# The sparse front of a graph and expert kernel: one-hots, keys, shifts and layer norm rewritten

## The reference

```python
edge_index = stack([src, dst])              # 41250 edges, sorted by dst; 1250 nodes
x = x + gnn(layernorm(x), edge_index, ...)  # x: 1250 x 512
x = x + moe(layernorm(x), ...)              # 512 tokens, 8 experts, 2 of them each

def gcn_conv(x, W, b, src, dst, n):
    h = x @ W.T
    s, d = concat(src, arange(n)), concat(dst, arange(n))   # own loop added
    deg = zeros(n).at[d].add(1.0); dinv = deg ** -0.5
    out = segment_sum(h[s] * (dinv[s] * dinv[d])[:, None], d, n)
    return out + b
# gnn: gcn_conv(512->128), relu, gcn_conv(128->64), then a decoder 64->128->256->512
# layernorm: (x - mean) / sqrt(var + 1e-5), no scale and no shift
```

## Time and profile before

| | us |
|---|---|
| median of 3 runs | 245.8 (245.12 to 248.06) |
| profiled execution | 245.55 |
| its span, first to last instruction | 243.8 |

### The profile page before, as it was taken

The page is one execution under the profiler, slowest core; times in us unless marked ns, Lnnn a source line. Parts: engine busy times, 40 slices in busy tenths (PEclk is TensorE's granted clock), DMA queues, the critical chain, the costliest instruction groups (busy, mean ns, idle before and its releaser), DMA issues.

```text
span 243.8 us, 3869 instructions
## 1 busy us (share of the span) xinstructions
PE 193.7 (79%) x1297; PEld 146.8 (60%) x1303; DVE 146.5 (60%) x292; ACT 105.0 (43%) x224; POOL 39.3 (16%) x50
## 2 busy tenths in 40 slices
PE   2371579999998888799999999978999999993000
PEld 2371369999997777765575544435977777771000
DVE  2919995766769881596560226865398667541224
ACT  3823974766743342630150342702587666440000
POOL 8600000000000000000010060057334400000750
PEclk9999999999999998589999999997799999999555
DMA  5999995000000000000000000424223921113573
GB/s 140 360 285 372 368 365 178 3 0 3 0 3 0 0 0 4 4 3 0 3 0 3 0 3 0 153 80 126 82 56 118 307 93 56 56 63 104 157 219 143
DMA packets 16011, 23.82 MB, mean 98 GB/s; under 512 B 3086, under 2 KB 7952, under 8 KB 15988
## 3 DMA queue, kind: packets, MB, share of 16 engines
q1 hardware_dynamic: 14354, 18.64, 22.9%
q0 software_dynamic: 1536, 4.72, 7.0%
q10 hardware_dynamic: 98, 0.17, 0.2%
HBM read 17.29 MB, written 6.23 MB: 96 GB/s over the span
## 4 chain that ended last, share of the span: by engine, by line
PE 71%; DVE 11%; DMA 7%; issue 5%; POOL 3%; ACT 1%; POOLq 1%; ACTq 0%; DVEq 0%
PE bank L1196 14%; PE bank L1266 11%; PE bank L1405 10%; PE bank L1432 5%; PE bank L1178 4%; PE bank L1191 4%; PE bank L1416 3%; PE bank L1435 3%; PE bank L1376 3%; PE bank L1417 2%; POOL at L526 2%; PE bank L1167 2%; DVE at L553 2%; DMA at<-y_rows,slot_i 2%; DVE ring L597 2%
## 5 line engine op out<-in xcount | busy, mean ns | idle before, releaser
L1196 PE MATMUL bank<-ring 128*128 128x120 bf16 x324 | 42.8, 290 | 0.0
L1196 PEld LDWEIGHTS bank<-ring 128*128 128x128 bf16 x324 | 35.2, 118 | 3.2 <-issue 0.6
L597 DVE TENSOR_TENSOR ring<-iota_quad,src_lo 128x1024 bf16<-128x1024 f16 x41 | 28.3, 690 | 13.9 <-PE bank L1202 13.3
L958 ACT CAST at<-bank 128x440 f32 (+1 forms) x41 | 21.9, 534 | 25.0 <-PE bank L1202 23.9
L1266 PE MATMUL bank<-at,ring 128*128 128x512 bf16 (+1 forms) x145 | 29.4, 345 | 0.5 <-issue 0.4
L597 DVE TENSOR_TENSOR ring<-iota_quad,key 128x960 bf16<-128x960 f16 x41 | 26.7, 651 | 0.0
L1191 PE MATMUL bank<-zeros_bf,ident_bf 128*128 128x440 bf16 (+1 forms) x41 | 15.3, 372 | 13.0 <-DVE ring L597 11.7
L1405 PE MATMUL bank<-at_r 128*128 128x512 f32 (+1 forms) x64 | 21.8, 404 | 0.0
L805 DVE TENSOR_TENSOR ew_r<-ew,at_r 128x1024 fp32r<-128x1024 f32 x16 | 19.3, 1216 | 0.0
L498 POOL MEMSET ring<- 128x640 bf16 x1 | 0.6, 632 | 114.3 <-PE bank L1272 114.3
L1266 PEld LDWEIGHTS bank<-at,ring 128*128 128x128 bf16 x150 | 13.6, 100 | 9.1 <-issue 1.1
(11 more groups left out here) (174 smaller groups left out, 346.3 us busy)
## 6 DMA issues: line engine op xcount, KB each, us to landing
ew<-in_w SPq DMA_DIRECT2D x16, 512.0 KB, 9.8
x_sb<-in_x SPq DMA_DIRECT2D x9, 256.0 KB, 4.9
out<-x_sb SPq DMA_DIRECT2D x9, 256.0 KB, 2.9
y_rows<-at SPq DMA_DIRECT2D x8, 256.0 KB, 2.1
wd3t_sb<-in_Wd3T SPq DMA_DIRECT2D x1, 512.0 KB, 5.3
x_rows<-xn SPq DMA_DIRECT2D x1, 512.0 KB, 2.8
x_rows<-at SPq DMA_DIRECT2D x1, 512.0 KB, 3.5
y_rows<-at SPq DMA_DIRECT2D x8, 64.0 KB, 2.3
```

Of the source, the lines that this page charges most:

```text
L597: last = v.tensor_tensor(hot[:, slot], lanes_quad[:, a:a + n].unsqueeze(1).to_broadcast([P, QUADS, n, QUAD]), of.rearrange("p (q t) -> p q ...
L958: nc.scalar.copy(at[:, :, bass.ds(column, wide)], bank[j][:, 0:CH * wide].rearrange("p (c n) -> p c n", c=CH)).then_inc(s_placed, 1)
L1196: last = mm(acc[:, :, bass.ds(shifts[g], WINDOW)], hot_src[:, j, t // QUAD, :, t % QUAD], hot_dst[:, j, t // QUAD, :, t % QUAD], start=Fal ...
```

## The change

It rewrites the work from the edges to `dinv`.

- One-hots are dense: one row of 128 or 80 elements per tile. Keys are held twice in a row (`lo2`, `key2`), so that comparisons read pairs.
- `WINDOW` is 8, each tile has its own shift, `WIDE` is 40, the last batch's 48. The first tile product starts the bank (`start=True`), without a product of zeros, except in the last batch. `at` is no longer cleared.
- Keys are made in rows by DVE as bf16 (`lo_row`, `key_row`, `carry_row`) and transposed by bf16 products; ACT and DVE spread them from PSUM. The first destinations of tiles are loaded by two DMAs of 4-byte pieces (`next_first`, `first_i`), which give shifts and columns.
- The checks for the general path are spread over POOL, DVE, ACT and PE.
- Layer norm is folded: the raw x is transposed and projected with weights whose column means are taken off (`w1c`, with a column of ones that gives the sum of x); ACT takes one sum of squares in place of two passes and a normalisation; the root of the variance is joined to that of the degree, and `h` is scaled with both (`norm_col`).
- 32 batches are unrolled, with a feature chunk for every three of them.
- `spread_dinv` runs inside the first aggregation, behind its first part. PE warms up with 16 products in place of 40.

```diff
-    WINDOW = 12
+    WINDOW = 8
-    WIDE = 44
-    WIDE_LAST = 2 * WINDOW
+    WIDE = 40
+    WIDE_LAST = 48
-    HEAD = 24
+    HEAD = 32
+    TRANSPOSED = [1 + 3 * c for c in range(CH)]
+    PROJECTED = [3 + 3 * c for c in range(CH)]
+    CENTRED = 2
...
 @block.sync
+            sp.dma_start(next_first[0:ROWS - 1, :],
+                         dst[rowlen:(ROWS - 1) * rowlen + 1:rowlen].rearrange("(r a) -> r a", a=1),
+                         allow_slow_non_contiguous=True).then_inc(s_next, 16)
...
 @block.gpsimd
-            nc.gpsimd.memset(at_flat, 0.0).then_inc(s_at_zero, 1)
...
 @block.vector
+            i_src, i_dst = edges[:, 0, :], edges[:, 1, :]
+            dve.wait_ge(s_src, 32)
+            link(v.tensor_scalar(hi_row, i_src, 0x1F80, 4, ALU.bitwise_and, ALU.logical_shift_right))
+            v.scalar_tensor_tensor(lo_row, hi_row, -16.0, i_src, ALU.mult, ALU.add).then_inc(s_lo_row, 1)
+            dve.wait_ge(s_dst, 32)
+            dve.wait_ge(s_next, 16)
+            v.tensor_copy(first_f[:, 0:ROWT], i_dst[:, 0:rowlen:P]).then_inc(s_first_f, 1)
...
+            for t in range(ROWT):
+                v.scalar_tensor_tensor(key_row[:, t * P:(t + 1) * P], i_dst[:, t * P:(t + 1) * P], first_f[:, t:t + 1],
+                                       hi_row[:, t * P:(t + 1) * P], ALU.subtract, ALU.add).then_inc(s_key_row, 1)
...
+                for hot, of, n, a in ((hot_src, lo, P, 0), (hot_dst, key, COLS, first)):
+                    last = v.tensor_tensor(hot[:, slot].rearrange("p t (n a) -> p t n a", a=2),
+                                           iota_slots[:, a:a + n].rearrange("p (n a) -> p n a", a=2).unsqueeze(1)
+                                           .to_broadcast([P, BATCH, n // 2, 2]),
+                                           of.unsqueeze(2).to_broadcast([P, BATCH, n // 2, 2]),
                                            ALU.is_equal)
...
+                    link(keep_keys(SOON, ROWS))
+                    dve.wait_ge(s_carryT, 1)
...
+                if b == 1:
+
+                    v.tensor_tensor(falls[:, 0:rowlen - 1], i_dst[:, 1:rowlen], i_dst[:, 0:rowlen - 1],
+                                    ALU.is_lt).then_inc(s_falls, 1)
...
+                if b == CENTRED:
+                    dve.wait_ge(s_colsum, 1)
+                    v.scalar_tensor_tensor(w1c[:, :, 0:HID], bank[7][:, 0:HID].unsqueeze(1).to_broadcast([P, KD, HID]),
+                                           -1.0 / D, w1t_sb[:, :, :], ALU.mult, ALU.add).then_inc(s_w1c, 1)
...
+            v.tensor_scalar(deg_std[:, 0], bank[3][:, 0:CH], 1.0, None, ALU.add).then_inc(s_deg_var, 1)
+            v.scalar_tensor_tensor(deg_std[:, 1], bank[3][:, 0:CH], 1.0, var_eps[:, :], ALU.add,
+                                   ALU.mult).then_inc(s_deg_var, 1)
...
 @block.scalar
+            act.dma_start(first_i[:, 0:FIRSTS], dst[0:(FIRSTS - 1) * P + 1:P].rearrange("(a n) -> a n", a=1),
+                          allow_slow_non_contiguous=True).then_inc(s_firsts, 16)
...
+                nc.scalar.activation(sweep[:, c % SWEPT], x_sb[:, c], ACT.Square, bias=x_sb[:, c, 0:1], scale=-1.0,
+                                     accum_out=square[:, c:c + 1]).then_inc(s_square, 1)
...
+                if b in TRANSPOSED:
+                    keep_transposed(TRANSPOSED.index(b))
+                elif b in PROJECTED:
+                    keep_h(PROJECTED.index(b))
+                elif b >= 2 and (b - 2) % 3 == 0:
+                    sum_squares((b - 2) // 3)
...
 @block.tensor
+            pe.wait_ge(s_lo_row, 1)
+            for t in range(ROWT):
+                last = mm(bank[2][:, t * ROWS:(t + 1) * ROWS], lo_row[:, t * P:(t + 1) * P], ident_bf[0:ROWS, 0:ROWS],
+                          start=True, stop=True)
...
-                    shift_i[0:1, bass.ds(b * BG, groups)], engines=[pe.engine], min_val=0, max_val=wide - WINDOW,
+                    shift_i[0:1, bass.ds(b * BATCH + 1, tiles - 1)], engines=[pe.engine], min_val=0, max_val=wide - WINDOW,
...
-                mm(acc, ident_bf[:, :], zeros_bf[:, 0:1].to_broadcast([P, CH * wide]), start=True, stop=False)
+                ends = wide != WIDE
+                if ends:
+                    mm(acc, ident_bf[:, :], zeros_bf[:, 0:1].to_broadcast([P, CH * wide]), start=True, stop=False)
...
+                for t in range(tiles):
+                    to = acc[:, :, bass.ds(shifts[t - 1], WINDOW)] if t else acc[:, :, 0:WINDOW]
+                    last = mm(to, hot_src[:, j, t], hot_dst[:, j, t], start=(t == 0 and not ends),
+                              stop=(first and t == tiles - 1), skip_group_check=not ends)
...
             neighbours([part[:, 0], part[:, 1], part[:, 2]], wait_part1, s_agg1,
-                       lambda i: product_h2(0) if i == 1 else None, before_last=rank_assignments)
+                       lambda i: product_h2(0) if i == 1 else None, spread_dinv, rank_assignments)
```

More of the change, by code:

```diff
@@ L166, in gnn_moe @@
         TP = NBATCH * BATCH
[L167 to L179, removed]
-        column_i = sb("column_i", [1, NBATCH], I32)
-        viol = sb("viol", [P, 5, GROUPS])
-        n_viol = sb("n_viol", [P, 8])
+        lo2 = sb("lo2", [P, TP, 2], FP16)
+        key2 = sb("key2", [P, TP, 2], FP16)
+        hot_carry = sb("hot_carry", [P, FULL_BATCHES, CH], BF16)
+        next_first = sb("next_first", [ROWS, 1], I32)
+        first_f = sb("first_f", [ROWS, ROWT + 1])
+        last_f = sb("last_f", [ROWS, ROWT])
+        first_i = sb("first_i", [1, TP], I32)
+        column_i = sb("column_i", [1, NBATCH], I32)
+        shift = sb("shift", [1, TP])
+        shift_i = sb("shift_i", [1, TP], I32)
+        NV = 3 * ROWT + 2
+        viol = sb("viol", [ROWS, NV])
+        NZ = FULL_BATCHES + 3
+        first_viol = sb("first_viol", [1, NZ + NV])
+        n_viol = sb("n_viol", [1, 1])
         slow_i = sb("slow_i", [1, 1], I32)
@@ L548, in _ @@
             v.memset(edges[PAD_ROW:ROWS, 1, LEFT:], N).then_inc(s_edge_pad, 1)
[L550 to L557, removed]
@@ L588, in _ @@
[L588 to L599 removed]
+            v.memset(next_first[PAD_ROW:ROWS, :], N + 1).then_inc(s_edge_pad, 1)
@@ new lines, in _ @@
+            last.then_inc(s_loT, 1)
+            for t in range(ROWT):
+                pe.wait_ge(s_key_row, t + 1)
+                last = mm(bank[3][:, t * ROWS:(t + 1) * ROWS], key_row[:, t * P:(t + 1) * P], ident_bf[0:ROWS, 0:ROWS],
+                          start=True, stop=True)
+            last.then_inc(s_keyT, 1)
+            pe.wait_ge(s_carry_row, 1)
+            mm(bank[6][:, 0:FULL_BATCHES], carry_row, ident_bf[0:ROWS, 1:2 * FULL_BATCHES:2],
+               start=True, stop=True).then_inc(s_carryT, 1)
@@ new lines, in column_sums, with sum_violations @@
+            def column_sums():
+                pe.wait_ge(s_w1, 16)
+                for k in range(KD):
+                    last = mm(bank[7][:, 0:HID], one[:, 0:1].to_broadcast([P, P]), w1t_sb[:, k],
+                              start=(k == 0), stop=(k == KD - 1))
+                last.then_inc(s_colsum, 1)
+            def sum_violations():
+                pe.wait_ge(s_viol, 7)
+                pe.wait_ge(s_fallen, 1)
+                mm(bank[5][0:1, 0:NV], one[0:ROWS, :], viol[:, :], start=True, stop=True).then_inc(s_violT, 1)
```

457 lines of the change are left out of this document (242 added, 215 removed).

## The result

The changed kernel is slower: 286.6 us median of 5 runs (286.5 to 287.9) against 245.1 (243.9 to 248.1); the ratio is 1.171, 95% interval 1.165 to 1.176. The forecast was 226, from 214 to 237. The profiled execution has a span of 286.1 us, where 243.8 + (226 - 245.8) = 224 were expected: 62 us too many. Two small steps, which the prediction priced by the nearest rows that it had, make up the 62: a copy of 4-byte pieces, and a load of seven registers in each of 40 batches.

What follows compares the result with a forecast made beforehand. PE's own queue was taken to bound the batches. From 245.55 us, 20.8 came off (last sum at 73.9, not 94.73), 0.5 and 0.3 were added: 225.55; the median lies 0.25 above, so 226, range 214 to 237.

Steps and rivals of the forecast that it cites:

- The load of seven registers: PE's queue, each batch: one load priced like that of four registers, 0.33 us, plus 0.03 more.
- 1.69 for a looped batch: PE's queue in the loop: 1.33 us of before, 3 x 0.11 and 0.03 more; eight such batches take 13.5.
- they land at 5.7 and 6.1: Front: the 4-byte copies `next_first` and `first_i`, issued near 2.0 and 2.4, land at these times, by the row of `gi_sb`.
- Rival C: A second load per batch, small DMAs that land late, or a clock that swings: 232 to 241 us; chance 0.12.
- A: The forecast itself: PE's queue sets 1.44 us a batch; 221 to 231 us; chance 0.60.
- B: PE's queue does not bind; ScalarE's and Vector's 1.05 to 1.1 us a batch do: 215 (212 to 219); chance 0.15.
- The clock: Thinner batches leave the array at 1.2 GHz: no cost in the batches, 2.2 us (0 to 2.8) in the aggregation.
- One-hots: Vector, each batch: the two one-hots take 1.00 us together, if the packed rate holds for rows of two.
- the flag: The flag `slow_i` that PE awaits before batch 3: there at 17.05 us, where batch 3 started at 32.14 before.
- 2.5 + 2.2: First aggregation: 2.5 us for spreading `dinv` inside it as 10 products, 2.2 for its start at the lower clock.
- the move of the spreading: `spread_dinv` moved into the first aggregation: -4.85 + 0.45 + 2.5 + 2.2 = +0.3 us.
- Last sum to first aggregation: Stretch behind the batches: two Vector steps add 0.5 us, `spread_dinv` leaves (-4.85), ScalarE's first part adds 0.45.

Runs made afterwards that it cites:

- seven aligned: The changed kernel with each batch's seven shifts stored and loaded from a multiple of eight on; 259.8 us in one run.
- eight registers: The changed kernel loading all eight shifts of a batch, the first (always 0) unused, from a multiple of eight on; 244.3 us, 0.997 of the kernel before.
- the repair: The changed kernel with the copy into `first_i` issued by SyncE ahead of the x loads, not by ScalarE; 276.9 us, 1.128 of the kernel before.
- without shifts: Eight-register loads and early `first_i` copy, then shifts dropped: each tile's product goes to a fixed place, PE loads no shifts; 206.2 us.
- with pairs: The changed kernel with early `first_i` copy and the old pairs: one shift for two tiles, 12 columns, four registers a load; 215.3 us, ratio 0.874.
- both repairs: The changed kernel with eight registers a load and the `first_i` copy issued ahead of the x loads; 235.7 us, 0.959 of the kernel before.

## Why the prediction was wrong

**What failed** is the step "The load of seven registers is not shown. Below, it costs what four cost; above, it becomes two loads, 0.40 more in each of 38 batches, 15 us." The load costs 1.37 us more, in 40 batches, and each batch shows it: the forecast 1.69 for a looped batch plus 1.34 is 3.03, and the steps inside an iteration of the loop are 3.06 to 3.19. In the sum the term is 40 x 1.34 = 54 us too small, of a measured miss of 61. The bound above was no bound. It supposed that a load has one price up to some number of registers. The rows of the two kernels and the runs give another law: 0.07 us, and 0.26 for each whole group of four counted from a start at a multiple of four, and 0.233 to 0.24 for each register left over, all of them where the start is not such a multiple (the only other start that was run is one place beyond it). One register 0.31, two 0.54, three 0.77, four 0.33 or 1.00, seven 1.70 or 1.06, eight 0.59. The one register is a flag that PE loads twice, far behind the batches, in the kernel before:

```profile
L381 PEldq TENSOR_LOAD <-path_i x2: 305/306/306, 125.5 to 125.9; - x2
```

The trace of before held the warning. Its loads are 327/332/544 ns, and the 544 is the last batch's, of two registers only. That half the work took longer would have shown that the price isn't one of number. I read the median of the form and not what stood at its maximum.

**The second failure** is "So they land at 5.7 and 6.1, just in time." `next_first` did, 2.9 us after its issue. `first_i` took 14.4 us (about 12.1 and 15.4 in the runs with seven aligned and with eight registers), and not the 3.7 of `gi_sb`. That row was near in size and far in place: `gi_sb` was issued at 13.88, behind the x loads on their own queue, `first_i` beside them from another. Full DMA engines alone do not explain it, for their busy share was 1.05 while `gi_sb` was under way, from 13.9 to 17.6. What makes the difference, the place or the queue, stays open, as the repair changed both. The prediction says of `s_next` that each microsecond more there moves everything by one; that holds, but for the other copy: 10.7 late, 9.5 lost. Put ahead of the x loads the copy took 4.9 (the DMA share from 4.0 to 7.3 was 0.42 and then 0.25, so it ran beside little), and batch 0 began at 10.32 against 10.4 foretold. The effect on the neighbour was missed too: the issue of `w1t` behind it, and with it ScalarE's copies; I had listed what the pieces wait for and not who waits behind them on their own queue.
Rival C, at 232 to 241 and a chance of 0.12, came nearest: it names small DMAs that land late, which is what happened, and a second load per batch, which is not. The trace has one load, with its registers fetched singly. C adds 6 to 15 us to the forecast where 61 came.

**What held.** The queue of PE as the bound of the batches (A against B): the runs without shifts and with pairs show it. The clock, at 0.64 in the head, cost nothing beside the queue that shows: 40 shorter loads are 44 us less by themselves, and with them 42.3 came back in all, though the clock rose too (0.83 from 30 to 60 us with eight registers). One-hots: 0.99 a batch where they follow each other, the rate of pairs holds. The start of batch 0 and the flag, once the copy is early: 10.32 for 10.4 and 15.8 for 17.05. The general path isn't taken. The clock stays at 0.50 from the looped batches into the aggregation (0.50 from 107.0 to 146.0). From the first aggregation product to the end the forecast added 2.5 + 2.2 = 4.7 to the 138.8 us of before; 143.4 is measured, 4.65 more. That the move of the spreading is worth about nothing is shown by its own run. Last sum to first aggregation was to take 6.4 and took 7.4: "issue" behind the degrees is 1.50 where 1.00 stood, ScalarE's first part takes 0.85 and not 0.45, and its last copy out of PSUM takes 0.58 where 0.38 stood.
Tile products were to lie less than 0.06 us apart. With a FUSED_REGOPS before each they lie 0.125 apart in a looped batch (eight in 1.00 us, clock 0.50); without shifts they lie 0.036 apart at full clock. So the forecast priced the array without the queue's part in it, and as the queue's own sum held that part, the time did not suffer.
With 0.59 for the load in place of 0.36, the prediction's own working gives 1.55 us for a plain batch of the head and 1.92 for a looped one; the run with both repairs has 1.62 and 1.95. Its sum would have been 226 + 40 x 0.23 = 235.2, and 235.7 is measured. That this is within 0.5 is in part luck: the flag came 1.3 earlier than foretold, and the stretch from it to the last sum took 1.4 longer. But the structure of the sum was right; one of its terms was mis-sized, and one wait ahead of it.

## What to carry to other kernels

Before an instruction is made larger, look at every size of it that the trace holds, the odd one at the end too; a price that falls or jumps between two sizes has steps, and the neighbours don't bound it. Where a chain of waits names two engines in turn and neither is busy, look at the queues: the one that came last need not be the one that was waited for. A tiny copy can take three times as long beside large ones (here 14.4 us against 4.9), and the next one on its queue can be held up with it: issue first what the first computation needs.

## What the runs showed of the hardware

TENSOR_LOAD of registers from SBUF goes in fours: 332 ns for four that start at a multiple of four, 1000 ns for the same four one element further, 591 for eight. The Trainium skill (Runtime: NRT & Kernel Launch, Instruction fetch mechanics) gives about 200 ns a register, for loads from HBM, even in bulk. The registers that are fetched singly here, from SBUF, lie near that, at 233 ns; a whole group of four, at 260 ns, is 65 a register, and there the measurement decides. 323 pieces of 4 bytes took 4.9 us issued ahead of 2.5 MB of x, and 14.4 issued beside it from another queue; the issue of 256 KB behind them on that queue then took 8.2 us in place of 0.4. A Vector operation from SBUF to SBUF lasted until GpSimd's clear had ended (5.25 us for a cast that takes 0.42 without the clear); copies out of PSUM beside the clear took 0.48 as ever.
